# The experts' down product as three products of rounded parts and remainders

## The reference, cut to what matters

```
z = 2.0 * buf
z = z * rsqrt(mean(z * z) + EPS) * norm_w
gu = einsum('ecd,ehd->ech', z, w13)          # 8 experts, 1024 outputs
g, u = split(gu, 2)                           # 512 and 512
y = buf + einsum('ech,edh->ecd', silu(g) * u, w2)   # the down product: 512 -> 192
```

## Time and profile before

| | before |
|---|---|
| median of 3 runs | 213.1 us (212.5 to 215.81) |
| the profiled execution's own time | 213.03 us |
| its span in the trace | 211.0 us |
| TensorE matmul busy | 191.9 us (91%) |
| VectorE busy | 125.0 us (59%) |
| ScalarE busy | 90.6 us (43%) |
| GpSimd busy | 67.8 us (32%) |

### The profile page before, as it was taken

One profiled execution on the slowest core, in us unless ns is written; L12 is line 12 of the kernel. 1 busy time (PEld: TensorE's weight loads), 2 busy tenths in 40 slices (PEclk: granted clock), 3 DMA queues, 4 the chain that ended last, 5 costly groups with the idle time before them and its releaser, 6 DMA issues.

```text
span 211.0 us, 4913 instructions
## 1 busy us (share of the span) xinstructions
PE 191.9 (91%) x1915; PEld 174.8 (83%) x1918; DVE 125.0 (59%) x381; ACT 90.6 (43%) x186; POOL 67.8 (32%) x114
## 2 busy tenths in 40 slices
PE   6879999999999998999999858499999999999970
PEld 1868998898998996998999633389999999999960
DVE  0267945857481156988765762556486477494174
ACT  2053630135345503366279451256567657643110
POOL 8531400112034000564656776000315414513000
PEclk9999999999999999999999999799999999999995
DMA  6999973014000000100100001266277668413713
GB/s 191 395 401 424 328 256 155 0 44 163 23 3 2 0 3 0 32 16 19 32 15 18 26 24 36 77 214 263 84 263 256 219 227 305 133 35 101 196 36 116
DMA packets 11204, 27.07 MB, mean 128 GB/s; under 512 B 2661, under 2 KB 6498, under 8 KB 9998
## 3 DMA queue, kind: packets, MB, share of 16 engines
q1 hardware_dynamic: 8366, 24.10, 32.9%
q0 software_dynamic: 2304, 2.21, 3.7%
q10 hardware_dynamic: 512, 0.46, 0.8%
HBM read 23.95 MB, written 5.77 MB: 141 GB/s over the span
## 4 chain that ended last, share of the span: by engine, by line
PE 75%; POOL 7%; DVE 6%; DMA 4%; issue 4%; ACT 1%; DVEq 0%; SPq 0%; POOLq 0%; ACTq 0%
PE ps L551 10%; PE ps L392 6%; PE ps L422 6%; PE ps L318 5%; POOL slots L818 4%; PE ps L536 4%; PE ps L537 4%; PE ps L538 3%; PE ps L533 3%; PE ps L532 3%; PE ps L372 2%; PE ps L375 2%; PE ps L374 2%; PE ps L376 2%; PE ps L373 2%
## 5 line engine op out<-in xcount | busy, mean ns | idle before, releaser
L843 POOL DMA_INDIRECT parts<-qT,toke x12 | 17.1, 1428 | 43.9 <-ACT qT L743 42.1
L818 POOL DMA_INDIRECT slots<-row,slot x16 | 17.9, 1120 | 29.5 <-issue 23.2
L981 DVE TENSOR_TENSOR wqkv<-raw,wqkv 128x1024 fp32r<-128x1024 f32 x16 | 19.5, 1221 | 7.6 <-DMA slots<-row,slot 4.4
L1056 DVE TENSOR_TENSOR v<-v,ps 128x246 f32<-128x246 f32 x32 | 12.5, 406 | 18.6 <-ACT v L731 18.6
L551 PE MATMUL ps<-xp,v 128*123 128x192 f32 x128 | 22.0, 326 | 0.0
L551 PEld LDWEIGHTS ps<-xp,v 128*123 128x123 f32 x128 | 20.6, 186 | 0.0
L637 ACT ACTIVATE prob<-sm 128x588 f32<-128x588 f32 x8 | 5.7, 706 | 31.1 <-DVE sm L902 31.1
L532 PE MATMUL ps<-zeA,wqkv 128*128 128x246 f32 x64 | 18.7, 292 | 0.0
L731 ACT ACTIVATE v<-ps 128x246 f32<-128x246 f32 x32 | 12.0, 375 | 14.2 <-PE ps L538 12.8
L536 PE MATMUL ps<-zeA,wqkv 128*128 128x246 f32 x64 | 17.9, 280 | 0.0
L538 PE MATMUL ps<-zeR,wqkv 128*128 128x246 f32 x64 | 17.8, 278 | 0.0
(11 more groups left out here) (143 smaller groups left out, 472.4 us busy)
## 6 DMA issues: line engine op xcount, KB each, us to landing
raw<-w SPq DMA_DIRECT2D x8, 1025.0 KB, 6.3
xp<-w SPq DMA_DIRECT2D x8, 384.0 KB
xp<-patches SPq DMA_DIRECT2D x8, 294.0 KB, 5.4
raw<-w_qkv SPq DMA_DIRECT2D x3, 768.0 KB, 6.7
slots<-blank SPq DMA_DIRECT2D x8, 196.0 KB, 4.6
xp<-slots SPq DMA_DIRECT2D x8, 196.0 KB, 6.6
parts<-zeros SPq DMA_DIRECT2D x1, 1176.0 KB, 8.4
part<-parts SPq DMA_DIRECT2D x4, 294.0 KB
```

What stands on the lines that cost most here:

```text
L818: P.indirect_dma_start(slots, bass.IndirectOffsetOnAxis(slot[:, p % PH, k:k + 1], 0), row[:, p % 2, k, :], None, bounds_check=EXPERTS * ST ...
L843: P.indirect_dma_start(parts, bass.IndirectOffsetOnAxis(toke[:, e, r:r + 1], 0), ye[0:EROWS, e % 2, r, :], None, bounds_check=TOPK * N + E ...
L981: last = V.tensor_tensor(wsp[:, j, 1, half, :], raw13[j][:, half * W13:(half + 1) * W13], wsp[:, j, 0, half, :].bitcast(f32), ALU.subtract)
```

## The change

`down(e)` becomes 24 matmuls of float32r: for each half r and block jt rounded gated values by rounded down weights, rounded gated values by the weights' remainder, and the gated values' remainder by rounded weights. The product of the two remainders is left out. For this

- ScalarE makes `hhi` (`inner_hi`, 128x246, four for each expert) and the rounded down weights (`split2_hi`, 128x768, one for each expert);
- VectorE makes `hlo` (`inner_lo`, 128x246, four for each expert);
- POOL makes the down weights' remainder (`split2_lo`, 128x768, one for each expert), the first two before its first send, those of experts 2 to 7 each at the head of the next pass of its loop, that is behind the two sends of the pass before;
- `hT` has one buffer instead of two, so gated(e, jt) waits for inner_hi(e-1, jt);
- SyncE loads the down weights of expert e+2 when both parts of those of expert e are made, in the same pass as the gate and up weights of expert e+2.

```diff
@@ SyncE, loop over e
-                if e >= 1:
-                    sp.wait_ge(down_done, 2 * e)
-                    load_w2(e + 1, 1 - j)
-            sp.wait_ge(down_done, 2 * (EXPERTS - 2))
-            load_w2(EXPERTS - 1, 1)
+                sp.wait_ge(w2hi_ready, e + 1)
+                sp.wait_ge(w2lo_ready, e + 1)
+                load_w2(e + 2, j)
@@ TensorE, down(e)
-                pe.wait_ge(hT_ready, JT * (e + 1))
-                pe.wait_ge(ld_d[j], 16 * (e // 2 + 1))
+                pe.wait_ge(w2hi_ready, e + 1)
+                pe.wait_ge(w2lo_ready, e + 1)
...
                     for jt in range(JT):
-                        last = mm(ps[0:EROWS, 6 + r, 0:D], hT[:, j, jt, r * EROWS:(r + 1) * EROWS], w2s[:, j, jt, :],
-                                  start=(jt == 0), stop=(jt == JT - 1))
+                        pe.wait_ge(hlo_ready, JT * e + jt + 1)
+                        mm(o, hhi[:, j, jt, c], w2t[:, j, 0, jt, :], start=(jt == 0), stop=False)
+                        mm(o, hhi[:, j, jt, c], w2t[:, j, 1, jt, :], start=False, stop=False)
+                        last = mm(o, hlo[j][:, jt, c], w2t[:, j, 0, jt, :], start=False, stop=(jt == JT - 1))
@@ ScalarE
+            def inner_hi(e, jt):
+                act.wait_ge(hT_ready, JT * e + jt + 1)
+                if e >= 2:
+                    act.wait_ge(down_done, 2 * (e - 1))
+                A(hhi[:, e % 2, jt, :], hT[:, jt, :], ACT.Copy).then_inc(hhi_ready, 1)
+
+            def split2_hi(e):
+                act.wait_ge(ld_d[e % 2], 16 * (e // 2 + 1))
+                if e >= 2:
+                    act.wait_ge(down_done, 2 * (e - 1))
+                A(w2t[:, e % 2, 0], w2s[:, e % 2], ACT.Copy).then_inc(w2hi_ready, 1)
...
             for e in range(EXPERTS - 2):
                 for jt in range(JT):
                     silu(e + 1, jt)
                     if jt < 2:
                         split_hi(e + 2, jt)
+                    if jt:
+                        inner_hi(e + 1, jt - 1)
+                inner_hi(e + 1, JT - 1)
                 x_hi(e + 2)
                 weigh(e)
+                split2_hi(e + 2)
@@ GpSimd
+            def split2_lo(e):
+                pool.wait_ge(w2hi_ready, e + 1)
+                P.tensor_tensor(w2t[:, e % 2, 1], w2s[:, e % 2], w2t[:, e % 2, 0].bitcast(f32), ALU.subtract).then_inc(w2lo_ready, 1)
+
+            for e in range(2):
+                split2_lo(e)
             for e in range(EXPERTS):
+                if 1 <= e < EXPERTS - 1:
+                    split2_lo(e + 1)
@@ VectorE
+            def inner_lo(e, jt):
+                if e >= 2:
+                    dve.wait_ge(down_done, 2 * (e - 1))
+                dve.wait_ge(hT_ready, JT * e + jt + 1)
+                dve.wait_ge(hhi_ready, JT * e + jt + 1)
+                V.tensor_tensor(hlo[e % 2][:, jt, :], hT[:, jt, :], hhi[:, e % 2, jt, :].bitcast(f32), ALU.subtract).then_inc(hlo_ready, 1)
...
                 for jt in range(JT):
                     gated(e + 1, jt)
                     if jt < 2:
                         split_lo(e + 2, jt)
+                    if jt:
+                        inner_lo(e + 1, jt - 1)
+                inner_lo(e + 1, JT - 1)
                 x_lo(e + 2)
```

More of the change, by code:

```diff
@@ L156, in vit_block @@
         vflat = v[:].rearrange("p a n -> p (a n)")
-        hT = vflat[:, 0:2 * JT * EC].rearrange("p (j t n) -> p j t n", j=2, t=JT)
+        hT = vflat[:, 0:JT * EC].rearrange("p (t n) -> p t n", t=JT)
         sg = vflat[:, 2 * JT * EC:2 * JT * EC + 4 * EC].rearrange("p (k n) -> p k n", k=4)
         qflat = qT[:].rearrange("p a b c d -> p (a b c d)")
-        ye = qflat[:, 0:4 * D].rearrange("p (j r d) -> p j r d", j=2, r=2)
-        part = sb("part", [PT, TOPK, PAIRS, D])
+        w2t = sb("w2t", [128, 2, 2, JT, D], f32r)
+        hhi = sb("hhi", [128, 2, JT, EC], f32r)
+        spare = (yA[:].rearrange("q c a n -> q (c a n)"), wqkv[:].rearrange("q w s c n -> q (w s c n)")[:, 8 * W13:])
+        hlo = [room[:, 0:JT * EC].rearrange("p (t n) -> p t n", t=JT) for room in spare]
+        ye = kT[:].rearrange("p a b c d -> p (a b c d)")[:, 0:4 * D].rearrange("p (j r d) -> p j r d", j=2, r=2)
+        part = qflat[0:PT, 0:TOPK * PAIRS * D].rearrange("q (k p d) -> q k p d", k=TOPK, p=PAIRS)
         ps = ctx.enter_context(nc.psum_tensor("ps", [128, 8, 512], f32))
@@ L194, in vit_block @@
         ld_part = [[sem(f"ld_part{k}{b}") for b in range(PARTS)] for k in range(TOPK)]
+        w2hi_ready, w2lo_ready, hhi_ready, hlo_ready = (sem(x) for x in ("w2hi_ready", "w2lo_ready", "hhi_ready", "hlo_ready"))
         member_ready, yohi_ready, yolo_ready, combined = (sem(x) for x in ("member_ready", "yohi_ready", "yolo_ready", "combined"))
@@ L549, in down @@
                         pe.wait_ge(ye_ready, 2 * (e - 1) + r + 1)
+                    o, c = ps[0:EROWS, 6 + r, 0:D], slice(r * EROWS, (r + 1) * EROWS)
                     for jt in range(JT):
-                        last = mm(ps[0:EROWS, 6 + r, 0:D], hT[:, j, jt, r * EROWS:(r + 1) * EROWS], w2s[:, j, jt, :],
-                                  start=(jt == 0), stop=(jt == JT - 1))
+                        pe.wait_ge(hlo_ready, JT * e + jt + 1)
+                        mm(o, hhi[:, j, jt, c], w2t[:, j, 0, jt, :], start=(jt == 0), stop=False)
+                        mm(o, hhi[:, j, jt, c], w2t[:, j, 1, jt, :], start=False, stop=False)
+                        last = mm(o, hlo[j][:, jt, c], w2t[:, j, 0, jt, :], start=False, stop=(jt == JT - 1))
                     last.then_inc(down_done, 1)
@@ L748, in _ @@
                 silu(0, jt)
+                if jt:
+                    inner_hi(0, jt - 1)
+            inner_hi(0, JT - 1)
+            for e in range(2):
+                split2_hi(e)
             for e in range(EXPERTS - 2):
@@ L758, in _ @@
                 silu(EXPERTS - 1, jt)
+                if jt:
+                    inner_hi(EXPERTS - 1, jt - 1)
+            inner_hi(EXPERTS - 1, JT - 1)
             weigh(EXPERTS - 1)
@@ L1055, in gated @@
                 dve.wait_ge(sg_ready, JT * e + jt + 1)
-                V.tensor_tensor(hT[:, e % 2, jt, :], sg[:, jt, :], ps[:, 2 + jt, EC:2 * EC], ALU.mult).then_inc(hT_ready, 1)
+                if e >= 1:
+                    dve.wait_ge(hhi_ready, JT * (e - 1) + jt + 1)
+                V.tensor_tensor(hT[:, jt, :], sg[:, jt, :], ps[:, 2 + jt, EC:2 * EC], ALU.mult).then_inc(hT_ready, 1)
+            def inner_lo(e, jt):
[4 more added lines that the diff above has]
+                V.tensor_tensor(hlo[e % 2][:, jt, :], hT[:, jt, :], hhi[:, e % 2, jt, :].bitcast(f32), ALU.subtract).then_inc(hlo_ready, 1)
             dve.wait_ge(v_done, PAIRS)
@@ L1078, in _ @@
                 gated(0, jt)
+                if jt:
+                    inner_lo(0, jt - 1)
+            inner_lo(0, JT - 1)
             for e in range(EXPERTS - 2):
@@ L1091, in _ @@
                 gated(EXPERTS - 1, jt)
+                if jt:
+                    inner_lo(EXPERTS - 1, jt - 1)
+            inner_lo(EXPERTS - 1, JT - 1)
             for i in range(2, len(ONCHIP)):
```

## The result

The changed kernel takes 237.1 us (median of 4 runs, 235.14 to 237.24), the kernel before in the same comparison 212.88; the ratio is 1.112 with an interval of 1.105 to 1.120. Slower, as forecast, but by 24 us and not 17: it lies above the range.

What follows compares the result with a forecast made beforehand. TensorE's queue was taken as the bound, passing to VectorE and ScalarE after the change; start 4.17, four cycles 10.52, down(6) 2.34 and down 0.10 us added 17.13 to 213.03, giving 230.2 us, range 219.5 to 233.5.

Steps and rivals of the forecast that it cites:

- The chain: Expert loop: ScalarE and VectorE, with added remainders, rounding and later x_hi, make the cycle 8.72 us against 7.63, +1.09 per expert.
- the hold: VectorE and POOL in the expert loop: split2_lo waits for split_lo 0, then makes split_lo 1 wait 1.54 us.
- rival (b): Expert loop: TensorE stays the bound and added operations fall into VectorE's idle time; 209.5 or 213.4 us, chance 0.08.
- TensorE's part: down(e): 24 matmuls 0.110 us apart take 2.65 us against 2.60, +0.05 us an expert, so no gain.
- the third fewer passes: down on TensorE: by the skill's weight-load rule too, fewer passes bring next to nothing, no less than 2.46 us.
- z: Expert loop: the moment x_lo of expert e is done, with TensorE waiting for it in the middle of its first block.
- the start: Before the loop's steady cycles: gate_up(2) as if 2.53 us later, plus split_lo 0 waiting 1.64 us for POOL; together 4.17.
- My upper bound for this term: split_lo's wait on POOL in the loop: at most 1.79 us, the whole of split2_lo; 0 if free.
- the cycle that ends in down(6): Late loop: down(6) waits for the scaled rows of down(5), starting 9.97 us after a gate_up instead of 7.63, +2.34.
- Rival (c): Expert loop: pauses lower TensorE's granted clock, or POOL's operation grows beside VectorE; 236 us and more, chance 0.07.
- My sum: Whole kernel: 4.17 start, 10.52 four cycles, 2.34 down(6) wait, 0.10 down; 17.13 onto 213.03 us, 230.2 us.

Runs made afterwards that it cites:

- experiment 1: Changed kernel without POOL's subtraction for the down weights' remainder, which is set to zero once: 221.25 us, ratio 1.030.
- experiment 2: Changed kernel with POOL's subtraction for expert e+2 put ahead of the sends of expert e: 225.81 us, ratio 1.055.
- experiment 10: Changed kernel with the down weights' subtraction on VectorE, in the loop behind x_lo(e+2), POOL keeping only its sends: 222.36 us, ratio 1.038.
- experiment 7: Kernel of experiment 6 with both split2_hi(0) and split2_hi(1) also put ahead of x_hi(0): 214.71 us, ratio 1.006.
- experiment 8: Kernel of experiment 7 with down as 16 plain float32 instructions on rounded values, both remainders made but unused: 215.4 us, ratio 1.011.
- experiment 3: Changed kernel with POOL's subtraction for experts 2 to 6 waiting until VectorE has ended split_lo 0: 233.12 us, ratio 1.085.
- experiment 9: Changed kernel with a one-column, one-input POOL operation and a semaphore wait between second send and subtraction, experts 2 and later: 233.42 us, ratio 1.095.
- experiment 11: Kernel of experiment 9 with the small POOL operation taking two inputs from SBUF instead of one: 232.02 us, ratio 1.089.
- experiment 12: Changed kernel with POOL's subtraction made a one-input operation that writes zeros, same place and columns: 225.57 us, ratio 1.058.
- experiment 5: Changed kernel with all four inner_hi(e+1) behind x_hi(e+2) and all four inner_lo(e+1) behind x_lo(e+2): 228.82 us, ratio 1.072.
- experiment 4: Changed kernel with each split_lo of 1024 columns as two operations of 512: 238.04 us, ratio 1.110.
- experiment 6: Changed kernel with the edits of experiment 2 and experiment 5 together: 216.07 us, ratio 1.016.

## Why the prediction came out as it did

**The chain, right.** The cycle without the hold was to be 8.72 us; experiments 1, 2 and 10 show 8.74, 8.74 and 8.73 in the cycles at full clock. That VectorE and ScalarE would take over as the bound, that gate_up would wait first for x_hi and then for x_lo, and that rival (b) would fail: all as the trace has it.

**TensorE's part, right.** I took 0.110 us between the matmuls of down, from the loads; the timeline of the changed kernel has 21 steps from 149.63 to 151.88, 0.107 each:

```profile
149.63 0.27 PE L558 MATMUL ps<-w2t,yA 128*123 128x192 f32 x1
...
151.88 0.27 PE L558 MATMUL ps<-w2t,yA 128*123 128x192 f32 x1
```

24 x 0.107 = 2.57 us against 2.60 before: nothing gained. Experiments 7 and 8 say so with TensorE as the bound. (What the prediction calls "the third fewer passes" stands in no row; the profile counts 16 instructions before and 24 after.) The Trainium skill ("TensorE: Matmul & The Clock Gate", section on LDWEIGHTS) would give 102.5 ns by the columns; the trace comes 5 ns from it.

**The hold, right in kind, wrong in its order and its size: the step that failed.** The step reads: "Then split2_lo waits for split_lo 0, which runs until 3.83, takes the place and holds it until 5.62, and split_lo 1, due at 4.08, waits 1.54 us." In the changed kernel split2_lo never waits for split_lo 0. In three of five cycles split_lo 0 did begin before the subtraction's row, but made no headway; in the other two it came 0.05 or 0.06 us behind and waited. It ended at z+6.43 (162.71 - 156.28), not z+3.83. With that, gated 1 came at z+6.35 instead of z+3.75, 2.60 later, and everything behind it followed at the forecast distances: z+11.31. In place of 1.54 the hold is 2.59 us a cycle. 1.54 is right where the order is as I wrote it and the clock is full: experiment 3 has two cycles of 10.29 us against my 10.26. Experiments 3 and 9, in which split_lo 0 gets through, take 1.8 and 3.2 us off the table's 95.5. At the start, beside POOL's second subtraction, the hold is as forecast: a row of 2.84 us, 1.62 more than 1.22, against 1.64.

My upper bound for this term was 1.79, the whole of POOL's operation, since I had the later one always wait for the earlier one. (My own rate of 2.04 ns a column gives 1.76 and not 1.79; measured were 1.84 to 1.86.) What I left out is that the earlier one can lose as well. The lost time is all the head start but some 0.13 us: 3.29 - 1.85 - 1.22 = 0.22 of 0.34, 3.77 - 1.84 - 1.22 = 0.71 of 0.83, and 4.02 - 1.85 - 1.22 = 0.95 of 1.07.

The Trainium skill ("SBUF — State Buffer", section on the two separate sides) has the lock as a matter of who starts first. Experiments 3 and 11 agree: the later operation waits to the end of the earlier one, now also a two-input operation of VectorE as the one that waits. The changed kernel does not agree: there in three of five cycles split_lo's row starts first, by 0.34 to 0.84 us, and POOL's operation is served first.

**The accounts.** The profiled execution took 237.07 us, 24.04 more than the 213.03 of before. Forecast 17.13. The four cycles are 11.31 each and not 10.26, +4.2; the cycle that ends in down(6) has the same hold, +1.05; the start comes out 0.2 later than forecast. That leaves 1.45 us, and they come from ahead of the experts: the first transposes of an expert's rows start at 136.42 and not at 134.97. The timeline of TensorE at the start of the kernel, before and after:

```profile
5.87 6.21 PE L318 MATMUL ps<-convw,xp 128*98 128x192 f32 x36 [0.95 <-DMA xp<-patches]
```

```profile
6.02 8.05 PE L321 MATMUL ps<-convw,xp 128*98 128x192 f32 x36 [1.11 <-DMA xp<-patches]
```

The same 36 matmuls of the first stage take 1.84 us longer, the longest of them 639 ns against 405, at a granted clock of 1.00 in both; why is open. It is not the change: the profiled executions of experiments 9, 11 and 12, which contain all of that stage unchanged, have these transposes at 134.83 to 134.88, and that of experiment 10 at 136.60.

**Rival (c)** named two ways to more than 233.5 us. The granted clock does fall, to 0.83, 0.66 and 0.86 in three stretches of the loop (154 to 164, 174 to 184, 194 to 204 us), and yet each cycle is 11.31 us. The cycle closes through POOL, not through TensorE: the scaled rows release the first send (167.89), the subtraction follows (171.06), then split_lo 0 (to 174.00), gated, x_hi, and the scaling again. So the clock's price is hidden in the changed kernel, and it shows in the other orders: 0.6 and 0.9 us in experiment 9, 0.9 in each of three cycles of experiment 3, 0.4 in each of two of experiment 5, 1.3 in the first of experiment 2 (10.00 against 8.74), 1.6 in the first of experiment 10. My sum put this term at nothing. Had the hold been as I wrote it, the clock would still have added 2.7 us: the five cycles of experiment 3 take 54.11 us, and five of 10.29 would be 51.45. And POOL's operation does not grow, 1.85 us against my 1.79; it is VectorE's that does. The 237.1 us lie where rival (c) put its time, 236 us and more, but neither of its ways led there.

**The range.** It left the hold at most 1.79 us. With 2.59 in place of 1.54 at the five places of the loop my sum is 230.2 + 5 x 1.05 = 235.4 us; the rest of the 237.1 is the 1.45 us from ahead of the experts and the 0.2 us of the start.

**What stays open.** Why the subtraction directly behind a send gets ahead of a split_lo that has begun, when a small operation at the same place does not. The rows show that it is settled before the subtraction's row begins (4), that a send alone doesn't do it (1), that neither one nor two inputs of a one-column operation do it (9, 11), and that a one-input operation of the same 768 columns doesn't either (12). What remains is an operation with two inputs and many columns; whether the number of columns decides, and from where on, was not tried. Nor was it tried whether an indirect DMA must stand ahead of the subtraction or any POOL operation would do; and experiments 9 and 11 put a wait on a counter in front of the subtraction together with the small operation, so they do not tell which of the two frees split_lo 0.

## What to carry to other kernels

Before a two-input elementwise operation goes to POOL because POOL has time, look at which two-input operations of VectorE it can meet there and whether VectorE is on the path: here 0.96 us of work in VectorE's idle time left the cycle at 8.73 us, and 1.85 us for each expert on idle POOL cost some 15 us in all. When two engines can hold each other up, bound the cost by the whole of the other's operation plus what one's own has done so far. When the new order lets TensorE pause in every cycle, give a lower granted clock a term in the sum: in the experiments it was worth 0.4 to 1.6 us in each cycle that it met. And put the operation on POOL where the other engine waits for something else, not directly behind an indirect DMA, as experiments 2 and 6 do. When three passes are to replace one product, compare the spacing of the passes with the old one first: at 0.107 us for 123 weight columns three passes and two float32 instructions cost the same, so there was nothing to win for the work put on the other engines.
